# Position-bias rows stored high beside low, filled by transfers with 32 outermost rows, and row maxima placed nearer to their fill

## What is computed

```
def _L0_conv_ref(x, w_qkv, b_qkv, w_proj, b_proj, rel_pos_h, rel_pos_w):
    ...
    rel_h = jnp.einsum('bhwc,hkc->bhwk', r_q, Rh)
    rel_w = jnp.einsum('bhwc,wkc->bhwk', r_q, Rw)
    attn_bias = (rel_h[:, :, :, :, None] + rel_w[:, :, :, None, :]).reshape(Bx * NUM_HEADS, S, S)
    scores = q @ jnp.swapaxes(k, -1, -2) * SCALE + attn_bias
    attn = jax.nn.softmax(scores, axis=-1)
    out = attn @ v
    ...
x = x + _L0_conv_ref(_gn(x), ...)
x = x + _L1_conv_ref(_gn(x), ...)
```

## Time and profile before

| | |
|---|---|
| median of 3 runs | 6088.66 us (6077.25 to 6094.65) |
| the profiled execution | 6093.63 us, span of its instructions 6091.8 us |
| PE busy | 4712.5 us, 77% of the span |
| DVE, ACT, POOL busy | 51%, 43%, 15% |
| mean granted TensorE clock | 0.861 of full speed |
| DMA | 386.23 MB, 63 GB/s over the span |

### The profile page before, as it was taken

The page is one execution under the profiler, slowest core; times in us unless marked ns, Lnnn a source line. Parts: engine busy times, 40 slices in busy tenths (PEclk is TensorE's granted clock), DMA queues, the critical chain, the costliest instruction groups (busy, mean ns, idle before and its releaser), DMA issues.

```text
span 6091.8 us, 97943 instructions
## 1 busy us (share of the span) xinstructions
PE 4712.5 (77%) x32598; PEld 2332.9 (38%) x32598; DVE 3078.8 (51%) x5558; ACT 2622.6 (43%) x3955; POOL 892.4 (15%) x1899
## 2 busy tenths in 40 slices
PE   3768877788777878777878777787778877778788
PEld 2233443444424444343433434434344443434334
DVE  2536555455554545544545454555545455545553
ACT  1333434344453444434445354444534445344454
POOL 3111100111101111011111111111011110111100
PEclk6777888888888988888889888888889889888898
DMA  5223221322213322123221223222133221332211
GB/s 102 61 59 74 49 70 55 80 64 63 56 49 80 71 62 65 39 75 76 70 62 46 72 63 77 64 58 64 50 80 69 63 65 36 80 76 70 57 35 32
DMA packets 231273, 386.23 MB, mean 63 GB/s; under 512 B 53788, under 2 KB 129120, under 8 KB 230752
## 3 DMA queue, kind: packets, MB, share of 16 engines
q1 hardware_dynamic: 184672, 266.11, 15.5%
q10 hardware_dynamic: 21504, 75.51, 6.3%
q0 software_dynamic: 24576, 37.80, 3.8%
HBM read 227.79 MB, written 88.08 MB: 52 GB/s over the span
## 4 chain that ended last, share of the span: by engine, by line
PE 40%; DMA 27%; SPq 23%; DVE 5%; issue 4%; ACT 2%; DVEq 0%; POOL 0%; ACTq 0%
DMA AR<-biases 15%; SPq L488 15%; PE P L1123 8%; PE P L1141 7%; PE P L1085 7%; DMA biases<-xn 6%; PE P L948 4%; PE P L949 4%; SPq L500 4%; DMA queries<-oraw 3%; DMA A<-mrow 3%; DVE mx L891 2%; SPq L475 2%; SPq L467 2%; PE P L1173 2%
## 5 line engine op out<-in xcount | busy, mean ns | idle before, releaser
L891 DVE TENSOR_REDUCE mx<-P 128x1 f32<-128x512 f32 x3072 | 1906.3, 682 | 1375.5 <-PE P L1085 1367.7
L761 ACT ACTIVATE probs<-P 128x1024 f32<-128x1024 f32 x1536 | 1505.4, 1022 | 1298.4 <-PE P L1141 1296.0
L1085 PE MATMUL P<-K,AR 96*128 96x256 f16 x6144 | 1163.0, 299 | 618.5 <-DMA AR<-biases 592.9
L777 ACT ACTIVATE probs<-P 128x320 f32<-128x320 f32 (+3 forms) x1632 | 638.9, 436 | 887.8 <-PE P L1194 545.5
L1085 PEld LDWEIGHTS P<-K,AR 96*128 96x128 f16 x6144 | 552.1, 104 | 1211.6 <-issue 398.9
L1141 PE MATMUL P<-AR,K 113*128 113x512 f16 x3072 | 951.2, 394 | 2.2 <-DVE mx L891 1.2
L1123 PE MATMUL P<-probs,V 128*17 128x512 f32 x6144 | 860.7, 634 | 9.9 <-ACT probs L761 9.9
L897 DVE TENSOR_REDUCE mxc<-P 128x1 f32<-128x336 f32 (+1 forms) x1536 | 646.5, 475 | 368.7 <-PE P L1094 368.4
L1061 PE MATMUL P<-QA,Z 128*128 128x64 f16 x3072 | 267.9, 253 | 302.9 <-DMA biases<-xn 225.4
L1141 PEld LDWEIGHTS P<-AR,K 113*128 113x128 f16 x3072 | 223.4, 99 | 716.8 <-ACT probs L761 528.9
L1194 PE MATMUL P<-A,K 113*128 113x320 f16 (+2 forms) x1536 | 467.5, 316 | 13.7 <-ACT probs L777 12.7
(11 more groups left out here) (120 smaller groups left out, 3740.5 us busy)
## 6 DMA issues: line engine op xcount, KB each, us to landing
AR<-biases SPq DMA_DIRECT2D x768, 128.0 KB
AR<-queries ACTq DMA_DIRECT2D x96, 512.0 KB
biases<-xn SPq DMA_DIRECT2D x192, 256.0 KB, 7.2
AR<-queries ACTq DMA_DIRECT2D x96, 256.0 KB
K<-oraw POOLq DMA_DIRECT2D x384, 64.0 KB, 4.7
xin<-in_x_dram SPq DMA_DIRECT2D x16, 768.0 KB, 9.4
queries<-oraw SPq DMA_DIRECT2D x384, 32.0 KB, 5.0
QA<-queries SPq DMA_DIRECT2D x192, 64.0 KB, 3.5
```

What stands on the lines that cost most here:

```text
L761: nc.scalar.activation(probs[:, u % RING, j:j + 2, :], P[:, b:b + 2, :], ACT.Exp).then_inc(p_done[0], 1)
L777: nc.scalar.activation(probs[:, full % RING, j, 0:n], P[:, step % SCORES[1], 0:n], ACT.Exp).then_inc(p_done[1], 1)
L891: V_.reduce_max(mx[:, n // 2, n % 2:n % 2 + 1], bank, AX.X).then_inc(used, 1)
L1085: last = mm(bank[:, QD * (v % 2):QD * (v % 2) + QD], AR[0:ROWS_MAX[0], part % SLOTS, v, c, j, 128 * q:128 * q + 128], K0[0:ROWS_MAX[0], h, ...
```

## The change

It has four parts.

1. The DRAM tensor `biases` changes its layout from (group, table, high/low, 32 rows, ...) to (group, table, 32 rows, high/low, ...), so the high and the low row of a position stand side by side. `biases_away` still issues four transfers of 256 KB; their DRAM side is now 32 rows of 8 KB at a stride of 16 KB, in place of one run.
2. `fill_slot` issues four transfers of 256 KB in place of eight of 128 KB. The source was (2 parts, 16 rows, 4 KB); it is 32 rows of 4 KB, each read twice for two variants. `PER_AR` counts six transfers in place of ten. The bytes of a fill, 1 MB, are the same.
3. The 0/1 rows of K0 are interleaved to match (static, once).
4. The maxima move. Phase 3: steps 27 to 43 become 23 to 41 (7 steps behind the fill at 16, in place of 11). Phase 4: 43 to 59 become 41 to 59. Phase 5 stays at 59. Layer 1's group 0, which ran in steps 10 to 27, is pressed into 10 to 23. In layer 1's attention the last group takes 0 to 25 in place of 26 and the next image's maxima begin at 25 in place of 30.

```
-    placed += evenly(max_jobs(0, image, 3), 27, 43) + evenly(max_jobs(0, image, 4), 43, 59)
+    placed += evenly(max_jobs(0, image, 3), 23, 41) + evenly(max_jobs(0, image, 4), 41, 59)
...
-        placed += evenly(max_jobs(1, i1, 0), 10, 27) + evenly(max_jobs(1, i1, 1), 77, 94)
+        placed += evenly(max_jobs(1, i1, 0), 10, 23) + evenly(max_jobs(1, i1, 1), 77, 94)
...
-    placed = evenly(max_jobs(1, image, 2), 0, 26)
+    placed = evenly(max_jobs(1, image, 2), 0, 25)
...
-    placed += evenly(early_maxes(n0), 30, STEPS[1] - TAIL)
+    placed += evenly(early_maxes(n0), 25, STEPS[1] - TAIL)
...
-        biases = nc.dram_tensor("biases", (G, 2, 2, 32, 4, GH, QD), F16).ap()
+        biases = nc.dram_tensor("biases", (G, 2, 32, 2, 4, GH, QD), F16).ap()
...
-        PER_Q, PER_K, PER_QA, PER_AR = 12 * 16, 12 * 16, 4 * 16, 10 * 16
+        PER_Q, PER_K, PER_QA, PER_AR = 12 * 16, 12 * 16, 4 * 16, 6 * 16
...
-                for r, n in ((0, 0), (16, 0), (32, 1), (48, 1)):
-                    sp.dma_start(K0[r:r + D, :, :],
+                for r, n in ((0, 0), (1, 0), (32, 1), (33, 1)):
+                    sp.dma_start(K0[r:r + 2 * D - 1:2, :, :],
...
-                        sp.dma_start(biases[g, table, s].rearrange("k a h n -> (k a) h n"),
+                        sp.dma_start(biases[g, table, :, s].rearrange("k a h n -> k a (h n)"),
...
-                for v in range(VAR):
-                    for table, first in enumerate((D * (v // 2), D * (v % 2))):
-                        src = biases[g, table, :, first:first + D, 2 * half:2 * half + 2, :, :]
-                        sp.dma_start(AR[32 * table:32 * table + 32, p % SLOTS, v, :, :, :],
-                                     src.rearrange("s k a h n -> s k (a h n)")).then_inc(ar_in[p], 16)
+                for table in range(2):
+                    for b in range(2):
+                        rows_ = biases[g, table, D * b:D * b + D, :, 2 * half:2 * half + 2, :, :]
+                        rows_ = rows_.rearrange("k s a h n -> (k s) (a h n)")
+                        same = slice(2 * b, 2 * b + 2) if table == 0 else slice(b, VAR, 2)
+                        sp.dma_start(AR[32 * table:32 * table + 32, p % SLOTS, same, :, :, :],
+                                     rows_.unsqueeze(1).broadcast_to((32, 2, 2 * GH * QD))).then_inc(ar_in[p], 16)
```

## The result

| | before | changed |
|---|---|---|
| median of 4 runs | 6088.04 us | 5128.49 us (5126.57 to 5133.88) |
| ratio, 95% interval | 1 | 0.8427 (0.8412 to 0.8441) |
| span of the profiled execution | 6091.8 us | 5126.3 us |
| PE busy | 4712.5 us, 77% | 4555.8 us, 89% |
| mean granted TensorE clock | 0.861 | 0.926 |

The forecast was 5123 us, in a range of 5020 to 5280. The change adds two lines in `fill_slot`, so L488 is now L490, L1085 is L1087, L1123 is L1125, L1141 is L1143.

The account below looks back on a forecast made before the run. PE bounds layer 0's attention between stalls on slow AR fills, so removed stalls return in full. 538 (layer 0) + 392 (layer 1) + 36 (images alone) = 966 us off 6093.6 gives 5128, corrected to 5123 us; range 5020 to 5280.

Parts of the forecast that it names:

- the signs it named: New profile: short DMA bursts near share 1, AR wait under 60 us, layer 0's attention about 147 us, layer 1's about 100.
- Two engines, 55 GB/s, 26.6 us a fill: AR bias fills: two outermost parts use 2 of 16 engines, 55 GB/s; a fill takes 26.6 us with 11 steps' cover.
- forecast 147: Slower rival, chance 0.03: fills stay on two engines, maxima start too early in both layers; 147 us more, 6236 us.
- 213 GB/s with 32 rows: AR fills: 32 outermost rows use 16 engines at 213 GB/s, as ACT's transfers do; 1.05 MB takes 4.9 us.
- 432 GB/s: AR fills: alternative rate of 16 engines at 27 GB/s each; fill 2.4 us, last 1 us stall gone, 16 us more gain.
- Stalls of layer 0 and the slow clock behind them: Layer 0's attention: 460 us of AR waits go, plus 110 us lost to PE's slower clock after stalls, over 16 images.
- Fill 3 with 1 us left of its stall: Layer 0, phase 3: fill lands about 2805.4, first maximum due about 1 us earlier; 1 us stall left, bounds 0 and 3.
- The pressed jobs share three banks with four rel jobs: Layer 0's attention: layer 1's 25 jobs pressed from 17 steps into 13 beside rel jobs; 1 us added, bounds 0 and 2.
- I cost the move of phases 3 and 4 at nothing: Layer 0's attention: where PE is the bound, moved maxima only change place; 33 jobs in 18 steps cost as in 16.
- Layer 1: 28 us: Layer 1's attention: 23.6 us of two stalls plus 4.3 of clock, 28 us an image, bounds 23.6 and 31; 392 over 14.
- only mixes scores into the same tie: Layer 1's attention: starting maxima five steps earlier gains nothing more, since PE and DVE are near a tie there.
- The wait for the biases stays: Rel jobs waiting for biases to land, 13 to 14 us an image, 225.4 in 16 waits: no change, 1 us a group either way.

## Why the prediction was right

The forecast of 5123 us was 5 us off. The mechanism was right, but that closeness is luck: in the traces layer 0's attention gave back 506 us over the 16 images where 538 were forecast, and layer 1's 430 over 14 where 392 were, so two misses of over 30 us cancelled. Of the signs it named, all came but layer 0's length, 150.2 us in place of about 147.

- **Two engines, 55 GB/s, 26.6 us a fill.** Right. The prediction leaves the 26.6 us beside its 19 us for 1.05 MB at 55 GB/s; most of the difference is some 4 us at the start in which the query transfers move their 0.79 MB. The runs with 4 and 8 outermost blocks show the engines following the count, and the placement alone shows what happens without the transfer: 160 us slower, forecast 147.
- **213 GB/s with 32 rows.** Right, read from ACT's transfers in the trace of before and met exactly. The 218 GB/s of the Trainium skill (SBUF — State Buffer, Door 1) pointed the same way. The 432 GB/s that 16 engines at 27 GB/s each would move do not occur in a fill.
- **Stalls of layer 0 and the slow clock behind them.** Right in size: 27.4 us of stalls and 6.9 of clock off 181.2 give 146.9, and the kernel with layer 0's old placement has 146.7. In the changed kernel it is 3.5 us longer, which is the price of the placement (the pressed jobs, below).
- **Fill 3 with 1 us left of its stall.** Right: 0.76 us in the image shown, and 18.6 in 14 waits over the run, of which 7.75 belong to layer 0's attention of the first image and 2.98 to the first image's jobs that run alone.
- **"The pressed jobs share three banks with four rel jobs, for which I add 1 us (bounds 0 and 2)."** This term was mis-sized: 6.0 us in the stage, outside its bounds, and 80 us over the run. The 1 us had no row behind it, and it left out both the waits on the banks, about 1 us each, and the longer stretch at the lower clock that goes with them.
- **"I cost the move of phases 3 and 4 at nothing."** It gives back 2.5 us in the image shown. Why was not tried; looser maxima leave PE more room in each unit, which would fit.
- **Layer 1: 28 us.** It was 30.6 (129.5 to 98.9). The 23.6 of stalls went; the maxima's region takes about 54 us where I had 53. That the start at step 25 "only mixes scores into the same tie" was wrong: it is worth 2.1 us an image, 30 us over the run, by the traces of the two kernels that differ in it.
- **The wait for the biases stays.** Right, 213.6 us against 225.4, and the new layout of DRAM did not slow it.

## What to carry to other kernels

When a DMA stalls an engine, look at the share of the DMA engines while it runs alone: 12.7% was the whole diagnosis, and the cure is the outermost size of both sides: eight in large transfers were enough here, and sixteen rows in small ones did as well. Then look at the rate with the share: engines that are all occupied and move 13 GB/s each are not the limit, and more of them would not help. And time the pieces of a change apart, because a placement tuned to a slow transfer is another matter once it is fast; here one line of the plan, added alone, cost 80 us beside a gain of 960.

## What the runs showed of the hardware that was not expected

- A transfer on two engines also held the queue that issued it: SP needed 26.76 us for 16 issues of 128 KB, and 10.37 and 11.10 us for 16 of the same size on four and on eight engines. An unrelated 8 KB transfer behind the fills (`A<-mrow`, one row) landed in a median of 12.3 us with two engines, 4.0 with four, 1.9 with eight and 1.8 with 16.
- Engines do not have a fixed rate: 26 to 27 GB/s each with two or four of them, 13 with 16 of them into 32 rows, 11 with eight in transfers of 64 KB into 8 rows. A share near 1 in the profile (96.6% at 213 GB/s) therefore does not mean that the engines are the limit.
